# An attention and mixture-of-experts kernel: scores and values as true fp32 matmuls on half tiles of the array

## The reference

```python
q = (hs @ wq.T).reshape(b, s, NH, HD).transpose(0, 2, 1, 3)      # NH 32, HD 64
k = (hs @ wk.T).reshape(b, s, NKV, HD).transpose(0, 2, 1, 3)     # NKV 8, each for 4 query heads
v = (hs @ wv.T).reshape(b, s, NKV, HD).transpose(0, 2, 1, 3)
q = _apply_rope(q, cos, sin)
k = _apply_rope(k, cos, sin)
scores = jnp.einsum('bhqd,bhkd->bhqk', q, k) / jnp.sqrt(jnp.float32(HD)).astype(hs.dtype)
scores = jnp.where(causal[None, None], scores, jnp.finfo(scores.dtype).min)
probs = jax.nn.softmax(scores, axis=-1)
o = jnp.einsum('bhqk,bhkd->bhqd', probs, v)
return o @ wo.T
```

## Time and profile before

| | |
|---|---|
| median of 3 runs | 942.84 us (942.55 to 943.8) |
| the profiled execution | 943.14 us |
| its span, first to last instruction | 941.3 us |
| attention, first maxima to last residual addition | 39.9 to 646.4 us |
| TensorE matmuls busy | 825.3 us |
| VectorE, ScalarE, GpSimd busy | 675.7, 525.0, 462.5 us |

### The profile page before, as it was taken

How to read it: one execution, slowest core, us unless ns; L and a number is a source line. 1 busy time by engine, 2 the same in 40 slices (tenths; PEclk the granted TensorE clock), 3 DMA queues, 4 the chain that set the end, 5 groups by cost and what they waited for, 6 DMA issues and landing times. The chain is left out here.

```text
span 941.3 us, 19141 instructions
## 1 busy us (share of the span) xinstructions
PE 825.3 (88%) x5639; PEld 748.5 (80%) x5639; DVE 675.7 (72%) x2295; ACT 525.0 (56%) x1617; POOL 462.5 (49%) x692
## 2 busy tenths in 40 slices
PE   3499999999999999999999999994503999999995
PEld 3388899999999999999999999984102788888884
DVE  5699888889888989888989888886594333333331
ACT  2277777776776776767777767673531232322221
POOL 2244555554545555556455555541771354455452
PEclk8599999999999999999999999998755999999998
DMA  6557536436255355363553653513863223233320
GB/s 186 118 133 148 92 68 101 99 71 113 68 92 90 80 99 96 78 101 72 99 96 63 118 93 72 103 46 105 249 215 121 33 45 51 45 56 50 52 46 7
DMA packets 77509, 86.35 MB, mean 92 GB/s; under 512 B 11392, under 2 KB 71040, under 8 KB 77152
## 3 DMA queue, kind: packets, MB, share of 16 engines
q1 hardware_dynamic: 65744, 73.65, 37.7%
q0 software_dynamic: 7488, 9.36, 6.0%
q10 hardware_dynamic: 4176, 2.11, 0.8%
HBM read 26.34 MB, written 9.32 MB: 38 GB/s over the span
## 5 line engine op out<-in xcount | busy, mean ns | idle before, releaser
L892 POOL TENSOR_SCALAR probs<-exps,inv_sums 128x128 f32<-128x128 f32 x256 | 96.6, 377 | 293.8 <-DVE inv_sums L726 239.5
L394 PE MATMUL scores<-kT,qT 128*128 128x256 f32 x1024 | 171.4, 290 | 15.3 <-DMA qT<-q_split 13.3
L564 ACT ACTIVATE exps<-masked,neg_max 128x128 f32<-128x128 f32 x256 | 102.9, 402 | 126.9 <-DVE neg_max L719 123.3
L394 PEld LDWEIGHTS scores<-kT,qT 128*128 128x128 f32 x1024 | 140.8, 192 | 19.1 <-DMA qT<-q_split 16.6
L731 DVE TENSOR_TENSOR pT_lo<-probsT,pT_hi 128x384 fp32r<-128x384 f32 x256 | 141.1, 551 | 0.6 <-ACT pT_hi L572 0.6
L404 PE MATMUL probsT<-tables,probs 128*128 128x128 f32 x768 | 126.1, 273 | 2.9 <-POOL probs L893 2.7
L566 ACT ACTIVATE exps<-masked,neg_max 128x256 f32<-128x256 f32 x256 | 126.8, 495 | 0.0
L893 POOL TENSOR_SCALAR probs<-exps,inv_sums 128x256 f32<-128x256 f32 x256 | 122.5, 478 | 0.0
L572 ACT CAST pT_hi<-probsT 128x384 fp32r<-128x384 f32 x256 | 117.9, 461 | 0.7 <-PE probsT L404 0.7
L1490 POOL DMA_INDIRECT out<-y,to_token x39 | 61.9, 1586 | 102.6 <-DVE y L1459 76.4
L719 DVE CUSTOM_DVE_ANT_0 masked<-scores,tables 128x256 f32<-128x256 f32 x256 | 107.4, 420 | 0.4 <-issue 0.4
(11 more groups left out here) (172 smaller groups left out, 2249.7 us busy)
## 6 DMA issues: line engine op xcount, KB each, us to landing
qT<-q_split SPq DMA_DIRECT2D x256, 128.0 KB, 3.5
kT<-k_split SPq DMA_DIRECT2D x128, 128.0 KB, 3.7
experts_w_out<-w_in SPq DMA_DIRECT2D x16, 512.0 KB, 3.9
raw<-w_attn SPq DMA_DIRECT2D x20, 256.0 KB, 3.6
experts_w_out<-w_out SPq DMA_DIRECT2D x2, 2048.0 KB, 8.2
out<-x_all SPq DMA_DIRECT2D x8, 256.0 KB, 3.2
xn_rows<-experts_w_out ACTq DMA_DIRECT2D x4, 512.0 KB, 4.8
x_all<-x SPq DMA_DIRECT2D x1, 1792.0 KB, 9.9
```

Source lines behind the costliest of these rows:

```text
L394: mm = nc.tensor.matmul(ps[:, tt * SEQ:(tt + 1) * SEQ], qT[:, g % 2, h, tt * P:(tt + 1) * P], kT[:, g // HALF, form, g % HALF, :], start=( ...
L564: nc.scalar.activation(exps[:, s, 0:P], masked[:, s, 0:P], ACT.Exp, bias=neg_max[:, s, 0:1], scale=-1.0, accum_out=sums[:, s, 0:1])
L892: nc.gpsimd.tensor_scalar(probs[:, h, 0:P], exps[:, s, 0:P], inv_sums[:, s, 0:1], 1.0, ALU.mult, ALU.mult)
```

## The change

Scores and values become true fp32 matmuls without splits, each on half of the array. For the scores, the even heads' 64 features lie on partitions 0 to 63 of `qT` and `kT`, the odd heads' on 64 to 127 (keys stand there twice): a matmul uses 64 rows of the array and 128 columns, and a pair writes two banks. There are four score banks now, all four heads are computed in one block at the start of a turn, and only the unmasked columns (128 and 256). For the values, a head's 64 output features are the 64 columns of its half: the even head writes partitions 0 to 63 of `heads_out`, the odd one 64 to 127. They belong to the turn two back and stand in one block behind the scores. `pT` is one fp32 copy, in two turns' buffers; `masked`, `exps` and `sums` have four buffers instead of two.

The banks for this come from elsewhere: q, k, v and the transposes of x share one bank, `x_bank` ("projected" in the profile), and `probsT` is one bank. So each projection waits until the one before has been read (`bank_read`, `next_q`, `other_projection`), and each set of transposes until the last one has been copied. `projects` says which projection stands beside q's in which turn. `xT_hi`, `xT_lo` and `rotated` are doubled. All `high_` and `low_` functions of q, k and v, and `probs_lo`, are gone; `copy_v` and `copy_probs` are plain copies.

```diff
-    qT = sb("qT", [P, 2, GROUP, SEQ], F32R)
-    kT = sb("kT", [P, 2, 2, HALF, SEQ], F32R)
-    masked = sb("masked", [P, 2, 3 * P])
+    qT = sb("qT", [P, 2, PAIRS, SEQ])
+    kT = sb("kT", [P, 2, HALF, SEQ])
+    masked = sb("masked", [P, GROUP, 3 * P])
...
-    q_bank, kv_bank = bank("q_bank"), bank("kv_bank")
-    s_bank = [bank("scores0"), bank("scores1")]
-    p_bank = [bank("probsT0"), bank("probsT1")]
+    x_bank = bank("projected")
+    s_bank = [bank(f"scores{h}") for h in range(GROUP)]
+    p_bank = bank("probsT")
...
+    def projects(b, g):
+
+        if g == 0 and b == 0:
+            return "v", 0, 0
+        if g in (1, 2):
+            return "kv"[g - 1], b, 1
+        if g in (3, 4, 6) and b < LAST:
+            return {3: "x", 4: "k", 6: "v"}[g], b + 1, 0
+        return None, 0, 0
...
         def move_q(m, s, first=False):
 
-            sp.wait_ge(q_hi, m + 1)
+            sp.wait_ge(q_rotated, m + 1)
...
+            for odd in range(2):
+                for a in range(2):
+                    at = odd * HD + a * 32
+                    sp.dma_start(qT[at:at + 32, s, :, :], rotated[odd:P:2, s, a, :]).then_inc(q_in[s], 16)
...
+        def next_q(b, g):
+
+            if past(b, g, 1):
+                bank_read(*back(b, g, 1))
+            else:
+                pe.wait_ge(q_parts, 2)
+            project_q(*ahead(b, g))
...
+        def scores(b, g):
...
+            for pair in range(PAIRS):
+                if n > 0:
+
+                    pe.wait_ge(s_read, (n - 1) * GROUP + 2 * pair + 2)
+                for tt in range(TT):
+                    for odd in range(2):
+                        rows = slice(odd * HD, odd * HD + HD)
+                        mm = nc.tensor.matmul(s_bank[2 * pair + odd][:, tt * SEQ:tt * SEQ + (tt + 1) * P],
+                                              qT[rows, g % 2, pair, tt * P:(tt + 1) * P],
+                                              kT[rows, g // HALF, g % HALF, 0:(tt + 1) * P], start=True, stop=True)
+                mm.then_inc(s_ps, 2)
...
         def prob_transposes(b, g, h):
...
+            i = turn_of(b, g) * GROUP + h
+            pe.wait_ge(probs_done, i + 1)
+            if i > 0:
+
+                pe.wait_ge(pT_done, i)
...
+            for pair in range(PAIRS):
+                for kt in range(TT):
+                    for odd in range(2):
+                        h = 2 * pair + odd
+                        rows = slice(odd * HD, odd * HD + HD)
+                        v = v_all[:, kt, g * HD:(g + 1) * HD]
+                        if kt == 0:
+                            mm = nc.tensor.matmul(o_bank[rows, pair * SEQ:(pair + 1) * SEQ], v, pT[:, n % 2, h, 0:2 * P],
+                                                  start=(pair == 0), stop=False, skip_group_check=True)
...
         def turn(b, g):
...
+            scores(b, g)
+            if past(b, g, 2):
+                values(*back(b, g, 2))
             if past(b, g, 1):
                 prob_transposes(*back(b, g, 1), 2)
             if prepares(b, g):
-                project_q(*ahead(b, g), 1)
-            if g == 5 and b < LAST:
-                x_transposes(b + 1)
-
-            scores(b, g, 1)
-            if past(b, g, 2):
-                output(*back(b, g, 2), 0)
+                next_q(b, g)
             if past(b, g, 1):
                 prob_transposes(*back(b, g, 1), 3)
             if past(b, g, 2):
+                output(*back(b, g, 2), 0)
+            prob_transposes(b, g, 0)
+            if past(b, g, 2):
                 output(*back(b, g, 2), 1)
...
+            other_projection(b, g)
             prob_transposes(b, g, 1)
...
+        def copy_probs(b, g, h):
+
+            n = turn_of(b, g)
+            act.wait_ge(pT_ps, n * GROUP + h + 1)
+            nc.scalar.copy(pT[:, n % 2, h, :], p_bank[:, 0:3 * P]).then_inc(pT_done, 1)
...
-        def probs_lo(b, g, h):
-
-            dve.wait_ge(pT_hi_done, turn_of(b, g) * GROUP + h + 1)
-            nc.vector.tensor_tensor(pT_lo[:, h, :], p_bank[h % 2][:, 0:3 * P], pT_hi[:, h, :].bitcast(F32),
-                                    ALU.subtract).then_inc(pT_lo_done, 1)
...
         def turn(b, g):
 
+            if g == 2 and b > 0:
+                add_out(b - 1)
             maxima(b, g, 0)
+            if past(b, g, 1):
+                what, of, half = projects(*back(b, g, 1))
+                if what == "x":
+                    x_lo(of)
+                if what == "k":
+                    rope_k(of, half)
+            if past(b, g, 1):
+                inverses(*back(b, g, 1), 3)
+            maxima(b, g, 1)
+            inverses(b, g, 0)
             if past(b, g, 2):
                 out_lo(*back(b, g, 2))
-            if past(b, g, 1):
-                probs_lo(*back(b, g, 1), 1)
+            maxima(b, g, 2)
             split_in_slot(b, g, 0)
-            inverses(b, g, 0)
...
+            inverses(b, g, 1)
             if prepares(b, g):
                 rope_q(turn_of(b, g) + 2)
             split_in_slot(b, g, 1)
```

More of the change, by code:

```diff
@@ L261, in move_k @@
             for a in range(2):
[L262 to L270 removed]
+                for copy in range(2):
+                    at = copy * HD + a * 32
+                    sp.dma_start(kT[at:at + 32, half, :, :], k_cos[:, a, :]).then_inc(k_in[half], 16)
         def turn(b, g):
@@ L387, in scores @@
-        def scores(b, g, h):
-            ps = s_bank[h % 2]
-            pe.wait_ge(s_read, turn_of(b, g) * GROUP + h + 1)
-            for tt in range(TT):
-                for form in range(2):
-                    mm = nc.tensor.matmul(ps[:, tt * SEQ:(tt + 1) * SEQ], qT[:, g % 2, h, tt * P:(tt + 1) * P],
-                                          kT[:, g // HALF, form, g % HALF, :], start=(form == 0), stop=(form == 1))
-            mm.then_inc(s_ps, 1)
+            for a in range(2):
+                mm = columns(b, piece, a)
@@ new lines, in project_k, with project_v @@
+            mm.then_inc(k_ps, 1)
+        def project_v(b, half):
+            piece = PIECES_ATTN.index(("v", half))
+            weights_split(b, piece)
+            for tt in range(TT):
+                n = 0
+                for k in range(KT):
+                    for x, w in ((xT_hi, w_hi), (xT_lo, w_hi), (xT_hi, w_lo)):
+                        mm = nc.tensor.matmul(x_bank[:, tt * SEQ:(tt + 1) * SEQ], x[:, b % 2, k, tt * P:(tt + 1) * P],
+                                              w[:, piece, k * 2 * P:(k + 1) * 2 * P],
+                                              start=(n == 0), stop=(n == 3 * KT - 1))
+                        n += 1
+            mm.then_inc(v_ps, 1)
@@ L405, in prob_transposes, with values @@
             mm.then_inc(pT_ps, 1)
[L407 removed]
+        def values(b, g):
             n = turn_of(b, g)
[L411 to L432 removed]
@@ L900, in turn @@
             divide(b, g, 0)
-            if g == 2:
-                rotate_k(b, 1)
-            if g == 6 and b < LAST:
-                rotate_k(b + 1, 0)
+            if past(b, g, 1):
+                what, of, half = projects(*back(b, g, 1))
+                if what == "k":
+                    rotate_k(of, half)
             divide(b, g, 1)
```

399 lines of the change are left out of this document (126 added, 273 removed).

## The result

The changed kernel takes **864.94 us** (863.98 to 868.09, four runs), the kernel before 942.69 us (941.76 to 943.8) on the same chip: a ratio of 0.9181, with a 95% interval from 0.9155 to 0.9206. The forecast was 878 us, 13 us more, with a range from 842 to 948.

A forecast was written before the change was run, and what follows sets the result against it. TensorE's queue was taken as the bound: a turn of 4.93 + 2.95 + 0.45 + 0.10 = 8.43 us against 9.35 saves 59 us over 64 turns, the start 6, giving 878 us; own range 840 to 910, wider range 842 to 948.

The forecast's parts named there:

- What bounds: Attention turns: each lasts as long as TensorE's queued matmuls, 9.35 us; other engines matter only where they hold TensorE up.
- What leaves and what stays: TensorE's turn: 28 fp32r score and value matmuls, 4.24 us, leave; pieces keeping their instructions stay at 4.93 us.
- The serial price: Scores and values as fp32 without overlap: 0.216 us for each 128 columns, 24 units, 5.18 us a turn.
- What the tiles give: Scores and values with paired tiles side by side: 2.95 us a turn, outer bounds 2.6 and 5.18.
- Changing the shape: TensorE's array changes shape three times a turn: 0.15 us each, 0.45 in all, bounds 0 and 1.05.
- The new waits: TensorE's waits for probs copies, oT_lo and the single projection bank: mostly free, 0.1 us a turn for lateness.
- The start: Before the first maxima: both splits leave VectorE's chain, so the maxima come 6 us earlier.
- Later stages: The end of the kernel: same pieces in another order, 0 us.
- Rival 1: Scores and values: no tiles run side by side, 1021 us; chance 0.12.
- Rival 2: Scores and values: only one kind overlaps, 945 to 954 us, or both in part, down to 910; chance 0.13.
- Rivals 3 and 5: 3: values' tile loads bare, 942 to 1006 us (0.05); 5: tiles at floor, shape changes free, 840 us (0.05).
- rival 4: Attention turns: TensorE no longer the bound, ScalarE's order makes it wait 0.5 us a turn, 910 us; chance 0.04.

The follow-up runs named there:

- the experiments that lengthened this queue: Changed kernel with scores on one tile (943.32 us), values on one tile (947.43), values' even heads first (909.2), transposes between scores and values (883.19), masked quarter computed (889.71).
- the runs on one tile: Changed kernel with even and odd heads on rows 0 to 63: scores alone 943.32 us, values alone 947.43 us, both 1025.85 us.
- the kernel with the values in a row: Changed kernel with a turn's value matmuls reordered, four of the even heads and then four of the odd ones: 909.2 us.
- all divisions of that kernel: Changed kernel plus four unused 128x512 additions at the end of VectorE's turn and one 128x512 copy on ScalarE: 913.65 us.

## Why the prediction was right, point by point

- **What bounds.** TensorE's queue, before and after: 0.08 us of idle time in a turn of 8.24, and the experiments that lengthened this queue came out close to the added time a turn times 64 (1.31 us as 78, 1.30 as 82, 0.71 as 44, 0.24 as 18, 0.41 as 25; by the product 84, 83, 45, 15, 26).
- **What leaves and what stays.** 8.24 - 3.22 - 0.08 = 4.94 us are left for the pieces that kept their instructions, predicted as 4.93. That these meet is in part luck: about 0.17 of the 4.94 is the wait for the probsT bank, which the prediction did not have, so the pieces themselves take about 4.8.
- **The serial price.** "0.216 for each 128 columns", read off the experts' fp32 matmuls, held: 2.82 and 2.75 us on one tile are 12 x 0.216 = 2.59, plus 0.23 and 0.16 about the changes of shape.
- **What the tiles give.** This term was mis-sized: 2.95 taken, 2.59 measured, the outer bound of 2.6. Four records of 256 columns, two on each tile, follow each other in 0.43 us, that is four units of 128 columns at 0.108 each, and the turn has 24 units. The floor of 2.8 from the issue of tiny transposes, 0.067 a record, was no floor: their price is their own, not that of issuing. The loads cost nothing either. The estimate of 3.3 us worked out from the Trainium skill, "TensorE: Matmul & The Clock Gate", section "Measured speedup vs the span model", was further off; with two tiles of fp32 the overlap was 2.0, not 1.57.
- **Changing the shape.** Also mis-sized, the other way: 3 x 0.15 = 0.45 taken, and 3.22 - 2.59 = 0.63 measured, 0.21 each; a fourth one cost 0.17 to 0.2. The rows from the routing stage gave 0.08 to 0.15, and the outer bound of 0.35 was not reached. The two errors together left 3.22 for 3.40.
- **The new waits.** Mis-sized: 0.10 taken, 0.08 of idle time measured and about 0.17 more, for the copy out of the single probsT bank, that the idle time doesn't hold. The prediction looked at this bank for head 3's transposes alone, and these do start without a wait (0.12 behind the projection, in all 64 cases between 120 and 560 us); those of heads 0 and 1 behind the output, which it did not look at, wait. The one it called the tightest, the output behind oT_lo, holds TensorE up for 2.2 us in all; the projection's single bank for 1.3, of which 0.9 are in one wait.
- **The start.** 6 taken, 7.6 measured. The splits did leave the chain: the first maxima now wait only for the layernorm's last step on VectorE. The scores are ready before, though their block took 2.9 us there, at a granted clock of 0.50, the lower of the two levels (1.2 GHz).
- **Later stages.** 0 taken, 1.5 measured, 0.5% of that stretch. Nothing in it was changed, and no run tells what it is.
- **The sum.** 68.9 - 59 = 10 from the turns, 1.6 from the start, 1.5 from the end: the 13 us by which 878 was too high. The errors within a turn had both signs (tiles 0.36 less than taken, the kept pieces about 0.15 less, shapes 0.18 more, waits about 0.15 more), so the turn came out 0.19 from its forecast, nearer than the largest term.
- **The rivals.** Rival 1 (1021 us) is what the kernel with both kinds on one tile does, 1026. Its break-even, 3.97 us of tiled work, can be checked as well: scores on one tile and values on two are 2.59 + 1.30 = 3.89, and that kernel stands at the time of before (1.0008). Rival 2 (945 to 954) is what one kind alone does: 943 and 947. Rivals 3 and 5 did not occur. Of rival 4 a small part did: TensorE waits for ScalarE's copies, but for about 0.17 us a turn and not 0.5, and it stays the bound; a large part came only with work that was added.

The prediction gave 0.24 to a loss, above all because no row of the trace showed two tiles at once. That was an open question at that time, and the runs on one tile show how much hung on it: the whole sign.

## What to carry to other kernels

Half-array matmuls in plain fp32 pay when two of them on different row or column tiles stand close together in the queue; alone they cost as much as full ones, so find out whether the partner is there before counting a gain. Interleave the tiles matmul by matmul, keep equal shapes together (a change of shape costs about 0.2 us), and look at the turn's budget on the bounding engine: here it gave the result within 2%. Cutting the columns from 256 to 128 shortens an fp32 matmul and not an fp32r one, so an edit that is worth nothing by itself can be a gain beside another. Where a buffer is given up, go through every user of it, and compare starts with the end of what releases them: a short wait hides behind matmuls that are still recorded as running.

## What the runs showed of the hardware

- Two fp32 matmuls on two row tiles (64x128) or two column tiles (128x64) run fully side by side. In a view of a short stretch of the changed kernel that ends 30 ns behind the start of the values, two records have started (one in the kernel with the values in a row):

```profile
308.69 0.44 PE L444 MATMUL heads_out<-pT,v_all 128*64 128x256 f32 x2
```

- TensorE started a matmul of a free tile ahead of three records of a busy one that had not started (7.5 us lost of an expected 50), but not ahead of seven.
- A change of the array's shape costs about 0.2 us (0.63 for three, 0.17 to 0.2 for a fourth).
- A GpSimd division of 128x128 out of SBUF took 1.33 us instead of 0.37, and one of 128x256 took 1.43 instead of 0.48, while VectorE added two SBUF operands (means over all divisions of that kernel 0.57 and 0.71, of the changed kernel 0.38 and 0.48). The Trainium skill, "SBUF — State Buffer", section "SBUF: two separate sides", describes a port pair that such a VectorE instruction holds as a whole, with the other engine blocked. The trace agrees in that the divisions beside the additions are about three times as long; whether GpSimd stood still all that time it doesn't show.
